# A mixture-of-experts layer: the experts' low-rank tile formed from weights laid side by side, one expert ahead, with weight splits in wider parts

## What is computed

```python
x0 = einsum('bct,bcd->bdt', x, weights[conditions]); xt = x0.reshape(1024, 256)
top_p, top_i = top_k(softmax(xt @ gate_w), 2)
for k in range(2):
    buf = tokens sent to each expert by choice k, 160 at most
    h = gelu(einsum('ecd,edf->ecf', buf, w1) + b1)
    y = einsum('ecf,efd->ecd', h, w2) + b2
    y = y + einsum('ecr,erd->ecd', gelu(einsum('ecd,edr->ecr', buf, wd)), wu)   # rank 32
    out = out + y[token's slot] * keep * top_p[:, k]
out = out + 0.2 * (gelu(xt @ sw1 + sb1) @ sw2 + sb2 + gelu(xt @ swd) @ swu)
return x + out
```

## Time and profile before

| | |
|---|---|
| median of 3 runs | 182.54 us (181.16, 182.54, 185.31) |
| span of the profiled execution, first to last instruction | 179.5 us |
| median less span (the profiled execution has no device time of its own on the page) | 3.0 us |
| PE busy | 174.6 us, 97% of the span |
| PEld, DVE, ACT, POOL busy | 170.0, 148.4, 145.8, 97.4 us |
| granted TensorE clock | 1.000 |

### The profile page before, as it was taken

One profiled execution on the slowest core, in us unless ns is written; L12 is line 12 of the kernel. 1 busy time (PEld: TensorE's weight loads), 2 busy tenths in 40 slices (PEclk: granted clock), 3 DMA queues, 4 the chain that ended last, 5 costly groups with the idle time before them and its releaser, 6 DMA issues.

```text
span 179.5 us, 4056 instructions
## 1 busy us (share of the span) xinstructions
PE 174.6 (97%) x1410; PEld 170.0 (95%) x1410; DVE 148.4 (83%) x332; ACT 145.8 (81%) x323; POOL 97.4 (54%) x110
## 2 busy tenths in 40 slices
PE   5999999999999999999999999999999999999994
PEld 6987789999989999999999999999999999999993
DVE  5678999999876779979789699798899889889822
ACT  3379799706779898997899799899899899898930
POOL 5802368210647662087977858958946455164700
PEclk9999999999999999999999999999999999999999
DMA  4594001669828492696878758579597868776242
GB/s 134 151 346 142 0 2 50 201 194 328 268 52 302 112 316 70 227 252 95 279 237 122 285 171 158 188 257 188 137 318 164 231 222 148 248 218 92 31 71 84
DMA packets 25885, 31.84 MB, mean 177 GB/s; under 512 B 4572, under 2 KB 22392, under 8 KB 25864
## 3 DMA queue, kind: packets, MB, share of 16 engines
q1 hardware_dynamic: 21720, 26.22, 45.5%
q0 software_dynamic: 3904, 5.25, 16.9%
q10 hardware_dynamic: 240, 0.10, 0.2%
HBM read 26.31 MB, written 5.24 MB: 176 GB/s over the span
## 4 chain that ended last, share of the span: by engine, by line
PE 88%; DVE 6%; ACT 3%; issue 1%; another core or an unknown queue 1%; POOL 0%; DVEq 0%; POOLq 0%; ACTq 0%
PE y_ps L1038 13%; PE y_ps L1040 13%; PE y_ps L1039 13%; PE hid_ps L1038 8%; PE hid_ps L1040 8%; PE hid_ps L1039 8%; PE turn_ps L1038 4%; PE turn_ps L1040 4%; PE turn_ps L1039 4%; PE y_ps L1046 2%; DVE w_l L703 2%; PE turn_ps L1207 2%; ACT gelu_f L627 1%; ACT hid_h L628 1%; PE hid_ps L1066 1%; PE turn_ps L1066 1%
## 5 line engine op out<-in xcount | busy, mean ns | idle before, releaser
L733 DVE TENSOR_TENSOR hid_l<-gelu_f,hid_h 128x320 fp32r<-128x320 f32 (+2 forms) x88 | 42.8, 501 | 13.8 <-ACT hid_h L628 13.4
L477 POOL DMA_INDIRECT out_rows<-y_row,slot_tok x23 | 38.2, 1662 | 26.8 <-DVE y_row L929 11.9
L463 POOL DMA_INDIRECT slot_in<-slot_rows,slot_src x23 | 33.0, 1435 | 18.5 <-DVE slot_src L889 8.2
L1038 PE MATMUL y_ps<-w_h,hid_h 128*128 128x256 f32 x128 | 36.4, 284 | 0.3 <-DVE hid_l L733 0.3
L1039 PE MATMUL y_ps<-w_l,hid_h 128*128 128x256 f32 x128 | 36.2, 283 | 0.0
L1040 PE MATMUL y_ps<-w_h,hid_l 128*128 128x256 f32 x128 | 36.2, 283 | 0.0
L1038 PE MATMUL hid_ps<-xs_h,w_h 128*128 128x256 f32 (+2 forms) x96 | 27.9, 291 | 0.0
L627 ACT ACTIVATE gelu_f<-hid_ps,bias_s 128x320 f32<-128x320 f32 x48 | 26.1, 543 | 1.9 <-PE hid_ps L1040 1.3
L1039 PE MATMUL hid_ps<-xs_l,w_h 128*128 128x256 f32 (+2 forms) x96 | 27.5, 287 | 0.0
L1040 PE MATMUL hid_ps<-xs_h,w_l 128*128 128x256 f32 (+2 forms) x96 | 27.5, 287 | 0.0
L710 DVE TENSOR_TENSOR w_l<-w_raw,w_h 128x512 fp32r<-128x512 f32 x40 | 26.6, 701 | 0.0
(11 more groups left out here) (239 smaller groups left out, 446.2 us busy)
## 6 DMA issues: line engine op xcount, KB each, us to landing
w_raw<-in_L_ffn_w SPq DMA_DIRECT2D x16, 1024.0 KB
w_raw<-in_L_ffn_sw SPq DMA_DIRECT2D x3, 1024.0 KB
x_in<-in_x SPq DMA_DIRECT2D x2, 512.0 KB, 3.7
w_raw<-in_L_ffn_sw SPq DMA_DIRECT2D x2, 512.0 KB, 7.1
slot_rows<-token_row SPq DMA_DIRECT2D x2, 512.0 KB, 4.1
wu_raw<-in_L_ffn_wu SPq DMA_DIRECT2D x24, 32.0 KB
out_rows<-base SPq DMA_DIRECT2D x1, 512.0 KB
slot_in<-slot_rows,slot_src POOLq DMA_INDIRECT x23
```

What stands on the lines that cost most here:

```text
L463: pool.indirect_dma_start(out=slot_in[par][0:n, s, :], out_offset=None, in_=x_rows, in_offset=bass.IndirectOffsetOnAxis(ap=slot_src[0:n, e ...
L477: pool.indirect_dma_start(out=out, out_offset=bass.IndirectOffsetOnAxis(ap=slot_tok[0:n, e, s:s + 1].bitcast(U32), axis=0), in_=y_row[0:n, ...
L733: dve.tensor_tensor(hid_l[:, j - 1, 0:n], gelu_f[:, j % 3, 0:n], hid_h[:, j - 1, 0:n].bitcast(F32), ALU.subtract).then_inc(hid_split, 1)
L1038: pe.matmul(out_ap, l_h, r_h, start=start, stop=False)
```

## The change

The low-rank tile of an expert is now one group of 4 matmuls: `wd_s` holds `wd`'s high part twice and its low part twice, side by side (128 output rows), and is multiplied by the tokens' high and low parts. ACT copies the lower half of the result (rows 64 to 127) to SBUF, DVE adds it to the upper half, ACT applies gelu twice and DVE subtracts. The tile of expert e+1 is made in period e, in the last tile of the second layer just before its step f = 2 (`LOW_MIDWAY`); only the first expert's is made at the start of its own period. Two buffers `low_s` and `low_b` take turns. On ACT and DVE, `w1` and `w2` are split in two parts of 1024 elements instead of four of 512, in the experts' periods; the tokens' split moves ahead of them, and the second half of `w2`, rather than its last quarter, is left to after tile 2 of the next period. The POOL copy of `wd` waits on another semaphore.

```diff
+WIDE = 2
+LOW_MIDWAY = 2
-        wd_h = [sb(f"wd_h{i}", [P, KD, 3, RANK], F32R) for i in range(2)]
-        wd_l = [sb(f"wd_l{i}", [P, KD, 3, RANK], F32R) for i in range(2)]
+        wd_s = [sb(f"wd_s{i}", [P, KD, 4, RANK], F32R) for i in range(2)]
...
+        low_b = sb("low_b", [P, SLOTS], F32R)
+        low_f = cond_g[0:2 * RANK, 0:SLOTS]
+        low_g = cond_g[0:RANK, SLOTS:2 * SLOTS]
+        low_of = [low_b, low_s]
...
             def wd_hi_part(v, par):
-                if v >= 2:
-                    pool.wait_ge(hid_made, hid_before(v))
+                if v > 2:
+                    pool.wait_ge(low_made, v - 2)
                 pool.wait_ge(wd_in, 16 * (v + 1))
...
+            def low_copy(e):
+                act.wait_ge(low_made, e + 1)
+                if e > 0:
+                    act.wait_ge(low_split, e)
+                act.activation(low_f[:, :], hid_bank(e + 2, 0)[2 * RANK:4 * RANK, 0:SLOTS], ACT.Copy).then_inc(low_copied, 1)
+            def low_gelu_part(e):
+                act.wait_ge(low_summed, e + 1)
+                act.activation(low_of[e % 2][0:2 * RANK, 0:SLOTS], low_f[:, :], ACT.Gelu)
+                act.activation(low_g[:, :], low_f[0:RANK, :], ACT.Gelu).then_inc(low_gelu, 1)
...
             def period(e, par):          # ACT
-                for j in range(HT):
+                if e == 0:
+                    low_copy(0)
+                for j in range(1, HT):
+                    if e == 0 and j == 2:
+                        low_gelu_part(0)
                     gelu_tile(e + 2, j, SLOTS, lambda f: bias_s[:, e, f:f + 1])
-                for c in range(CHUNKS):
-                    w1_chunk(e + 2, par, c)
-                    if c == 1 and e < E - 1:
-                        act.wait_ge(slots_turned, e * KD + 2 * KD)
-                        slots_hi_part()
-                for c in range(CHUNKS):
-                    w2_chunk(e + 2, par, c)
+                if e < E - 1:
+                    act.wait_ge(slots_turned, e * KD + 2 * KD)
+                    slots_hi_part()
+                for c in range(0, CHUNKS, WIDE):
+                    w1_chunk(e + 2, par, c, WIDE)
+                if e < E - 1:
+                    low_copy(e + 1)
+                w2_chunk(e + 2, par, 0, WIDE)
+                if e < E - 1:
+                    low_gelu_part(e + 1)
+                w2_chunk(e + 2, par, WIDE, WIDE)
...
+            def low_sum(e):
+                dve.wait_ge(low_copied, e + 1)
+                dve.tensor_tensor(low_f[:, :], hid_bank(e + 2, 0)[0:2 * RANK, 0:SLOTS], low_f[:, :],
+                                  ALU.add).then_inc(low_summed, 1)
+            def low_lo(e):
+                dve.wait_ge(low_gelu, e + 1)
+                low = low_of[e % 2]
+                dve.tensor_tensor(low[2 * RANK:LOW, 0:SLOTS], low_g[:, :], low[0:RANK, 0:SLOTS].bitcast(F32),
+                                  ALU.subtract).then_inc(low_split, 1)
...
             def period(e, par, rows=True):          # DVE
-                for j in range(HT):
+                if e == 0:
+                    low_sum(0)
+                for j in range(1, HT):
                     split_tile(e + 2, j, SLOTS)
+                    if e == 0 and j == 1:
+                        low_lo(0)
...
-                    if rows and 2 <= j < LATE_LO + 2:
-                        w2_chunk(CHUNKS - LATE_LO - 2 + j, 1 - par, e + 1)
-                for c in range(CHUNKS):
-                    w1_chunk(c, par, e + 2)
-                    if c == 1:
+                    if rows and j == 2:
+                        w2_chunk(CHUNKS - WIDE, 1 - par, e + 1, WIDE)
+                if e < E - 1:
+                    slots_lo_part(e + 1)
+                for c in range(0, CHUNKS, WIDE):
+                    w1_chunk(c, par, e + 2, WIDE)
+                    if c == 0:
                         if e + 2 <= E:
                             wd_part(par, e + 2)
                         wu_part(par, e + 2)
-                        if e < E - 1:
-                            slots_lo_part(e + 1)
+                if e < E - 1:
+                    low_sum(e + 1)
                 if e == 0:
                     sort_biases(slice(1, E))
-                for c in range(CHUNKS - LATE_LO):
-                    w2_chunk(c, par, e + 2)
+                w2_chunk(0, par, e + 2, WIDE)
+                if e < E - 1:
+                    low_lo(e + 1)
...
+            def low_tile(e, size):
+                par = (e + 1) % 2
+                pe.wait_ge(slots_lo, (e + 1) * KD)
+                pe.wait_ge(wd_lo, e + 2)
+                dst = hid_bank(e + 2, 0)[:, 0:size]
+                for k in range(KD):
+                    both = wd_s[par][:, k, :, :].rearrange("p g r -> p (g r)")
+                    pe.matmul(dst, both, xs_h[:, k, 0:size], start=(k == 0), stop=False)
+                    ins = pe.matmul(dst, both, xs_l[:, k, 0:size], start=False, stop=(k == KD - 1))
+                ins.then_inc(low_made, 1)
...
             def rows_out(e, par, size, midway):     # expert_out likewise, in its second tile
...
+                        if s == tiles[-1] and f == LOW_MIDWAY:
+                            midway()
...
                 for e, size in enumerate(sizes):
-                    pe.wait_ge(slots_lo, (e + 1) * KD)
-                    for j in range(HT):
+                    if e == 0:
+                        low_tile(0, size)
+                    for j in range(1, HT):
                         hidden(e + 2, j, other, e + 1, xs_h, xs_l, slice(0, size), size)
...
+                    ahead = (lambda: low_tile(e + 1, sizes[e + 1])) if e < E - 1 else (lambda: None)
```

More of the change, by code:

```diff
@@ L142, in build @@
         x_in = sb("x_in", [P, NT, D])
[L143 removed]
+        cond_g = sb("cond_g", [P, C * C])
         cond_diag = sb("cond_diag", [P, NT, P])
@@ L316, in held_by @@
         def held_by(u, j):
-            tiles = [i for i in range(1 if u == LAST else 0, j) if hid_banks(u)[i] is hid_banks(u)[j]]
+            tiles = [i for i in range(1 if u > 1 else 0, j) if hid_banks(u)[i] is hid_banks(u)[j]]
             return tiles[-1] if tiles else None
@@ L574, in w2_chunk @@
                         act.wait_ge(y_made, y_before(v))
-                act.activation(w2_h[par][:, c * FT:(c + 1) * FT, :], w2_raw[:, c * FT:(c + 1) * FT, :],
-                               ACT.Copy).then_inc(w2_hi, 1)
+                rows = slice(c * FT, (c + n) * FT)
+                act.activation(w2_h[par][:, rows, :], w2_raw[:, rows, :], ACT.Copy).then_inc(w2_hi, n)
             act.wait_ge(warm_set, 1)
@@ L1108, in hidden @@
                 if j == 0:
-                    pe.wait_ge(wd_lo, v + 1)
-                if u < 2 and j == 0:
+                    pe.wait_ge(wd_lo, 1)
                     pe.wait_ge(gate_lo, 1)
@@ L1165, in expert_out @@
                 cols = slice(m * P, (m + 1) * P)
-                pe.wait_ge(hid_split, hid_count(e + 2, 0))
-                pe.matmul(dst, wu_s[par][:, cols], low_s[:, 0:size], start=True, stop=False)
+                pe.wait_ge(low_split, e + 1)
+                pe.matmul(dst, wu_s[par][:, cols], low_of[e % 2][:, 0:size], start=True, stop=False)
                 for f in range(NF):
+                    if f == LOW_MIDWAY:
+                        midway()
                     if m == 0:
@@ L1173, in expert_out, with rows_out @@
                 ins.then_inc(y_made, 1)
-            def rows_out(e, par, size):
+            def rows_out(e, par, size, midway):
                 v = e + 1
@@ L1295, in experts @@
                         turn_slots(e + 1, other, (sizes[e + 1] + P - 1) // P)
+                    ahead = (lambda: low_tile(e + 1, sizes[e + 1])) if e < E - 1 else (lambda: None)
                     if e < ROWS_FROM:
-                        for m in range(KD):
-                            expert_out(e, m, other, size)
+                        expert_out(e, 0, other, size)
+                        expert_out(e, 1, other, size, ahead)
                     else:
-                        rows_out(e, other, size)
+                        rows_out(e, other, size, ahead)
                 last_quarter()
```

78 lines of the change are left out of this document (43 added, 35 removed).

## The result

| | before | after |
|---|---|---|
| median of the runs | 182.5 us (181.16 to 185.31, 6 runs) | 188.95 us (188.78 to 189.04, 6 runs) |
| profiled execution: span, device time | 179.5 us, no time of its own | 187.3 us, 189.04 |
| PE busy | 174.6 us | 174.4 us, but 93% of a longer span |

What follows compares the result with a forecast made beforehand. PE bound the kernel before; afterwards the loop over ACT bounds all seven periods. Four early periods +3.0, three late +3.6, end -0.1 take the span from 179.5 to 186.0; with 3.04 around it 189.0 us, range 184.0 to 192.0.

Steps and rivals of the forecast that it cites:

- E: Moment in each expert's period when ACT's last gelu has issued and the next work starts; the prediction counts times from it.
- The tile waits for `wd`'s low part: PE idles at the low-rank tile until DVE's `wd` subtraction ends: 1.4 us in late periods, some 8 us in all.
- The terms of the path: Instructions before the low-rank tile: ACT's 1024 copy, pitch 0.95; DVE's 1024 subtraction, pitch 1.14; `wd`'s low part, 0.29 us.
- T: Moment when PE starts the low-rank tile, predicted at E + 3.2 us.
- ACT's loop: ACT idles 1.5 us before copying the low-rank tile; `w2`, gelus and the next expert queue behind that wait.
- Tile 7: Its gelu waits for DVE because `w2`'s part after tile 2 is wider: 0.54 us per expert from e = 1 on.
- G: Start of the next expert's first gelu on ACT, predicted at E + 7.04 us in a late period.
- Two `y_t` copies in early periods: On ACT before G while e < 4, they add 0.88 us, making an early period 15.06 us against 14.18 late.
- PE's 2.0 us less work: The low-rank tile goes from 6 matmuls to 4 for eight experts, 16 matmuls of about 0.125 us less on PE.
- Rival 1: `wd`'s low part arrives before PE asks, so only PE's saved matmuls show: 180.5 us, chance 0.13.
- Rival 2: The wider `w2` part after tile 2 is absorbed, minus 7 x 0.54 = 3.8 us: 185.2 us, chance 0.15.
- Rival 3: DVE's low-rank sum is late for ACT's gelus too, some 0.4 us per period, 2.8 more: 191.8 us, chance 0.12.

Runs made afterwards that it cites:

- e2_quarter: Changed kernel with only a quarter of `w2` behind tile 2 on DVE, the third quarter moved to the end of its order: 185.46 us, ratio 1.025.
- e9_last_later: Changed kernel with the `low_of_last` call moved from the end of the second expert's splits to the end of that period: 188.99 us.
- e8_copy_later: Changed kernel with ACT's low-rank copy behind the first wide part of `w2` and its low-rank gelus behind the second: 186.07 us, ratio 1.027.
- e1_wd_first: Changed kernel with `wd`'s subtraction moved ahead of the wide parts of `w1` on DVE: 186.54 us, ratio 1.034.
- e6_wide_only: Kernel before with only `w1` and `w2` split in two parts in the experts' periods, nothing else of the change: 181.82 us, ratio 1.003.
- e5_sum_first: e3_both with the low-rank sum moved ahead of the second part of `w1` on DVE: 179.80 us, ratio 0.993.
- e10_best: e5_sum_first with the `low_of_last` call moved to the end of the second expert's period: 179.54 us, ratio 0.994.
- e3_both: Changed kernel with the edits of e1_wd_first and e2_quarter together: 182.64 us, ratio 1.012.
- e4_mid7: Changed kernel with the low-rank tile made before step f = 7 instead of f = 2, 15 matmuls later: 193.31 us, ratio 1.069.

## Why the prediction was right, and where its sum was off

Predicted 189.0, measured 188.95. The mechanism was right, but agreement to 0.05 us is luck; two errors cancel. The span came out at 187.3, not 186.0, and around it lay 189.04 - 187.3 = 1.74 us, not the 3.04 that I took from the kernel before. That 3.04 was the median of three runs less a span of another execution, and those runs were high: beside the experiments the kernel before had 180.8 to 180.9. In spans the change costs 7.8 us, where my sum had 6.5.

The period that the prediction reads as e = 5 was that of e = 6, as said above; its sums count from E and don't change by it. Step by step:

- **The tile waits for `wd`'s low part: right.** Seven waits, 7.0 us in all, where I said some 8: 0.45, 0.98, 0.58 and 0.89 us in the early periods, then 1.25, 1.24 and 1.59. In the second of them lies the omitted term below.
- **The terms of the path.** ACT's pitch of 1024 elements was 0.95 as taken, DVE's 142.46 - 141.31 = 1.15 (1.14), `wd`'s subtraction 0.29. Two hand-overs were left out: DVE starts 0.10 after the first high part ends (140.12 + 1.09 = 141.21), and PE starts 0.14 after `wd_s` ends (142.75) where I had 0.04. So T was E + 3.41, not E + 3.2. This is the mis-sized term: 0.2 us in each late period. The Trainium skill, "ScalarE: Activation LUTs", section "What ACT_TABLE_LOAD costs", states 186 ns + 0.833 ns per element and an overlap of 93 ns, from which I had estimated 1.04 us and a pitch of 0.95 for the 1024 copy. In the trace the pitch is 0.95. The duration is 1.05 us for `w2` (line 587), near the page, and 1.09 for `w1` (line 578), the copy on this path, nearer to my 1.10. Either way the two hand-overs were larger than the difference.
- **ACT's loop: right.** The copy started at E + 4.15 (4.0), the next expert's first gelu at 146.71 - 139.48 = E + 7.23 (7.04), after an idle 1.48 (1.5).
- **Tile 7: right.** From G to the next E 153.87 - 146.71 = 7.16 (7.14). e2_quarter shows the 0.5 us alone.
- **Two `y_t` copies in early periods.** Their pitch together was 117.94 - 117.29 = 0.65 and not 0.88, which took back the hand-overs: 15.04 to 15.11 measured, 15.06 predicted. The earlier trace rows has 0.91 for such a pair, this row 0.77: the second copy follows the first 0.14 sooner. And I took a copy's duration for its pitch.

```profile
117.29 0.77 ACT L710 ACTIVATE y_t<-y_ps 128x320 f32<-128x320 f32 x2
117.94 0.53 ACT L638 ACTIVATE gelu_f<-turn_ps,bias_s 128x320 f32<-128x320 f32 x1
```

- **An omitted term.** `low_of_last` in e = 1, +0.87. I read one late period and carried it to all seven. Shown in the profile of e9_last_later.
- **An open one.** The period of e = 6 was 14.74, 0.35 over its neighbours. DVE started its first wide part 156.06 - 154.50 = 1.56 us behind ACT's, in e = 5 1.19. The profile names ACT's copy, which had ended 0.5 us earlier. In this period e2_quarter, e8_copy_later and e9_last_later have the same late start (1.55 to 1.59) and e1_wd_first has not, so it goes with the kernel's order and not with one execution. What held it stays open.

```profile
156.06 1.23 DVE L738 TENSOR_TENSOR w_l<-w_raw,w_h 128x1024 fp32r<-128x1024 f32 x1 [0.73 <-ACT w_h L578]
```

Together the seven periods were 104.66 us against 102.8 predicted: 0.88 from e = 1, 0.56 from e = 6 (0.2 of it hand-overs), 0.4 from the other late ones. The prologue gave back 0.7: E of e = 0 came at 63.95 instead of 64.66. No run shows that the change did that. In e6_wide_only, which has the prologue of the kernel before, E came at 63.36, and in e5_sum_first at 65.76.

- **PE's 2.0 us less work: seen in the late periods only.** The busy time of the whole program doesn't show it: 174.4 in the changed kernel, 175.1 in e5_sum_first, 172.2 in e10_best, with the same matmuls in all three. That e10_best comes near the 172.6 predicted is mostly luck, since 1.35 of its 2.4 us under the kernel before lie ahead of E of e = 0. The stages are plainer. From E of e = 4 to E of e = 7, where PE hardly stops, the kernel before takes 38.98 us, e5_sum_first 38.20 and e10_best 38.19: 0.26 per expert, as the sum had it (0.25). From E of e = 0 to E of e = 4 they take 57.24, 57.48 and 57.01, so there next to nothing is gained. In these two stretches together PE's busy time is 97.16 us in the changed kernel and 95.11 in e10_best; the stops seem to add to it, which no run tests.

**The rivals.** Rival 1 (only PE's relief shows) is what the change does once the three places in DVE's order are mended: e5_sum_first and e10_best are 0.6% to 0.7% faster, 1.1 to 1.2 us by the medians, a bit over half of PE's 2.0. Rival 2 (the wide part is absorbed) fell in the changed kernel and holds, but for some 1 us, in e6_wide_only, where PE bounds. Rival 3 (a late low-rank sum) wasn't in the changed kernel, but came out in e1_wd_first and e3_both. The prediction had the sum ready only 0.1 us before ACT asks for it, so it had to come out once ACT asks earlier; my expectations for the two kernels ignored that. The failed step there is that I removed one bound without asking again which stands next.

## What to carry over

- When a piece of work is moved ahead to hide it, its inputs get earlier due times. Look for each input in the in-order list of the engine that makes it, and count what stands ahead of it. Here the tile had 2.3 us of cover for `wd`'s low part, the move took all but 0.15 of it, and the wider part and the tokens' copies in front of it made the input 1.0 us later (E + 3.27 instead of E + 2.24).
- The wait that the profile puts down to one engine may be paid on another. e4_mid7 has no wait of PE for `wd` and is the slowest of all; what counts is when the in-order engine behind it, ACT, gets its input.
- Merging parts saves a small fixed share each, and delays whoever waits for the first half. It costs little while another engine bounds (e6_wide_only, ratio 1.003), and costs its whole extra length when the loop through the parts bounds (e2_quarter against the changed kernel).

## What the runs showed that I had not expected

Three bounds stood close behind each other: the wait for the tile, the wait for the sum and the stall at tile 7. Late periods in the order in which these were removed: 14.39 us in the changed kernel, 13.90 without the stall at tile 7, 13.50 with `wd` moved too, 12.56 to 12.95 with the sum moved as well. So each edit took 0.4 to 0.9 us off. The first two edits together left the kernel 1.2% slower than before; only with the third is it faster, by 0.7%.
